# Second adder of a four-part kernel: four pairs of taps summed on VectorE, a ring of six, and side work moved to GpSimd and to the last stage

## The reference

```python
x = x + L0_conv(ln_c(x))        # 1x1 conv, adder 1x1, bn, relu, 3x3 conv, adder 3x3, bn, relu
t = t + L0_ffn(ln_t(t))         # a scan of up to 33 steps, each chooses an operation by argmax
x = x + L1_conv(ln_c(x))        # two quantised 3x3 convolutions
t = t + L1_ffn(ln_t(t))         # spectral filters (16 of them), mixed by M_phi, and M_u terms
```

```python
# out[n,co,h,w] = -sum over ci and 9 taps of |x_patch - w[co,ci,kh,kw]|
for kh in range(3):
    for kw in range(3):
        xs = xp[:, :, kh:kh + 28, kw:kw + 28]
        acc = acc - jnp.abs(xs[:, None] - w[None, :, :, kh, kw, None, None]).sum(axis=2)
```

## Time and profile before

| | |
|---|---|
| median of 3 runs | 366.26 us (362.93 to 367.12) |
| span of the profiled execution | 364.3 us; no time of its own beside the span is given for it |
| median less span | 2.0 us |
| PE busy | 346.7 us (95%) |
| DVE busy | 215.8 us (59%) |
| ACT busy | 178.7 us (49%) |
| POOL busy | 21.2 us (6%) |
| second adder, from the first unit to PE's last matmul | 39.07 to 138.54 us |
| last part, PE's filters and mixing | from 258.5 us to the end |

### The profile page before, as it was taken

The page is one execution under the profiler, slowest core; times in us unless marked ns, Lnnn a source line. Parts: engine busy times, 40 slices in busy tenths (PEclk is TensorE's granted clock), DMA queues, the critical chain, the costliest instruction groups (busy, mean ns, idle before and its releaser), DMA issues.

```text
span 364.3 us, 11456 instructions
## 1 busy us (share of the span) xinstructions
PE 346.7 (95%) x5077; PEld 212.4 (58%) x5077; DVE 215.8 (59%) x329; ACT 178.7 (49%) x180; POOL 21.2 (6%) x44
## 2 busy tenths in 40 slices
PE   8899999999999999899999998698999999999996
PEld 6437457743333345554663343465777778788884
DVE  2789999999999995455936785265211111111112
ACT  2862997887887952264828774312211111111110
POOL 4481000000000002000000000000000000000000
PEclk9999999999999999999989999999999999999999
DMA  5718300000000006400000000000230000000001
GB/s 171 222 21 266 122 2 2 2 3 2 2 2 0 2 2 234 137 7 12 1 2 2 3 1 2 7 0 2 67 71 2 4 4 4 4 4 2 4 4 46
DMA packets 10320, 13.12 MB, mean 36 GB/s; under 512 B 4106, under 2 KB 8988, under 8 KB 10264
## 3 DMA queue, kind: packets, MB, share of 16 engines
q1 hardware_dynamic: 9288, 9.11, 8.1%
q0 software_dynamic: 832, 3.00, 2.5%
q10 hardware_dynamic: 144, 0.20, 0.2%
HBM read 10.70 MB, written 0.40 MB: 30 GB/s over the span
## 4 chain that ended last, share of the span: by engine, by line
PE 57%; DVE 27%; SPq 7%; issue 4%; DMA 2%; ACT 2%; DVEq 0%; ACTq 0%
PE PS L989 57%; DVE pool_ L822 17%; SPq L238 3%; DMA W1R<-in_fwa 1%; DVE TMP L786 1%; DMA W4R<-in_aw 1%; SPq L232 1%; DVE pool_ L932 1%; DMA WA2R<-in_wa2r 1%; SPq L241 1%; SPq L243 1%; DVE pool_ L819 1%; SPq L245 1%; DVE MSC L735 0%; ACT pool_ L495 0%
## 5 line engine op out<-in xcount | busy, mean ns | idle before, releaser
L989 PE MATMUL PS<-pool_,CON 128*32 128x392 f32 (+2 forms) x1320 | 111.4, 493 | 0.7 <-ACT pool_ L495 0.2
L989 PEld LDWEIGHTS PS<-pool_,CON 128*32 128x32 f32 (+1 forms) x1320 | 49.0, 110 | 60.8 <-issue 43.7
L443 ACT ACTIVATE pool_<-TMP,WA 128x3136 f32<-128x3136 f32 x26 | 75.4, 2930 | 11.0 <-PE PS L989 10.8
L822 DVE TENSOR_SCALAR pool_<-TMP,WA 128x3136 f32<-128x3136 f32 x44 | 79.5, 1847 | 0.1
L977 DVE COPY pool_<-PS 128x392 f32<-128x392 f32 x32 | 18.1, 566 | 82.5 <-PE PS L989 82.5
L544 ACT ACTIVATE pool_<-PS 128x392 f32<-128x392 f32 x32 | 15.9, 498 | 83.3 <-PE PS L989 83.3
L989 PE MATMUL PS<-pool_,WS 128*32 128x392 f32 (+3 forms) x1024 | 46.6, 333 | 0.0
L989 PE MATMUL PS<-HE,WS 128*32 128x392 f32 (+3 forms) x1024 | 46.5, 333 | 0.1
L989 PEld LDWEIGHTS PS<-pool_,WS 128*32 128x32 f32 x1024 | 37.0, 110 | 10.0 <-issue 0.8
L989 PEld LDWEIGHTS PS<-HE,WS 128*32 128x32 f32 x1024 | 36.5, 111 | 10.7 <-issue 1.6
L989 PE MATMUL PS<-CON 128*128 128x196 f32 (+1 forms) x142 | 28.2, 337 | 1.1 <-DVE QZ L626 0.5
(11 more groups left out here) (237 smaller groups left out, 323.0 us busy)
## 6 DMA issues: line engine op xcount, KB each, us to landing
pool_<-in_pho SPq DMA_DIRECT2D x1, 3144.0 KB, 11.9
HE<-in_phe SPq DMA_DIRECT2D x1, 3136.0 KB, 11.8
QZ<-CW SPq DMA_DIRECT2D x12, 98.0 KB, 2.2
CW<-in_cw POOLq DMA_DIRECT2D x2, 576.0 KB, 4.8
CON<-in_con POOLq DMA_DIRECT2D x1, 732.5 KB, 5.6
out_y<-Y SPq DMA_DIRECT2D x1, 392.0 KB, 2.4
CQ<-in_ws SPq DMA_DIRECT2D x16, 9.0 KB
MPP<-in_mpp POOLq DMA_DIRECT2D x1, 256.0 KB, 3.1
```

Source lines behind the costliest of these rows:

```text
L443: a.activation(unit, window(n // CQ), ACT.Abs, bias=WA2[:, n:n + 1], scale=-1.0).then_inc(s["act_unit"], 1)
L822: v.tensor_scalar(unit, window(n // CQ), WA2[:, n:n + 1], None, ALU.max).then_inc(s["dve_unit"], 1)
L989: return t.matmul(out_, lhsT, rhs, start=start, stop=stop, skip_group_check=True)
```

## The change

Nine taps by eight groups were 72 groups; now c8 = 7 of taps 0 and 1, 2 and 3, 4 and 5, 6 and 7 are summed on DVE into one unit each, so PE sums 68 groups (n = 0..67). The pair stands where the odd tap's c8 = 7 stood, at n = 14, 29, 44 and 59. DVE makes the first tap's unit as before (L831 of the changed kernel), waits for it (`pair_half`), and then adds max(x, w) of the second tap in place with one `scalar_tensor_tensor` for each image (L834, 128 x 784). The second adder's ring has six slots, the sixth in `QZ`. Off DVE go: `u_mixers` and `mixers(1, .)` to DVE's own evictions of the last part (u = 1 to 9), `biases`, `quantised` and the key table to POOL; ACT's last quantising step goes to POOL and its `MUL` copies into the last part (u = 16). Steps 4 and 5 of `mixers(0, .)` move from ahead of the second adder into it (n = 10, 12).

```diff
+RG2 = 6
-NG = CQ + 9 * CQ
-ON_ACT = [on_scalar(g % CQ) for g in range(NG)]
+PAIRED = CQ - 1
+PAIRS = {1: 0, 3: 2, 5: 4, 7: 6}
+GROUPS = [((0,), c8) for c8 in range(CQ)]
+GROUPS += [((PAIRS[tap], tap) if c8 == PAIRED and tap in PAIRS else (tap,), c8)
+           for tap in range(9) for c8 in range(CQ) if not (c8 == PAIRED and tap in PAIRS.values())]
+NG = len(GROUPS)
+ON_ACT = [on_scalar(c8) for taps, c8 in GROUPS]
...
-        AMF = HSUM[:, 0:NOPS * NB]; KEYT = sb("KEYT", [P, NOPS * NB])
+        AMF = sb("AMF", [P, NOPS * NB]); KEYT = sb("KEYT", [P, NOPS * NB])
...
+        def slot(g):
+            n = g % RG if g < CQ else (g - CQ) % RG2
+            return RING[:, n, :, :] if n < RG else QZ[:, :, :]
...
# GpSimd, behind the padding of Y2R
+            g.wait_ge(s["mask_in"], 32)
+            gl(g.tensor_copy(AMF[0:1, :], AMT[0:1, :]))
+            gl(g.tensor_scalar(KEYT[0:1, :], FMT[0:1, :], 2.0, None, ALU.mult))
+            gl(g.tensor_tensor(KEYT[0:1, :], KEYT[0:1, :], AMF[0:1, :], ALU.add))
+            gl(g.tensor_scalar(AMF[0:1, :], KEYT[0:1, :], 0.0, None, ALU.is_gt))
+            gl(g.tensor_tensor(per_op(AMF), per_op(AMF), b4, ALU.mult))
+            g.tensor_tensor(per_op(KEYT), per_op(KEYT), per_op(AMF), ALU.add).then_inc(s["key_ready"], 1)
             g.wait_ge(s["ring_free"], NG)
             g.memset(H1P[:, :], 0.0).then_inc(s["pads"], 1)
+            g.wait_ge(s["decided"], 1)
+            g.wait_ge(s["q_sc"], 1)
+            for src, dst, i in ((CW1, CQ1, 0), (CW2, CQ2, 1)):
+                gl(g.tensor_scalar(src[:, :], src[:, :], QS[:, 2 + i:3 + i], 1.0, ALU.mult, ALU.mult))
+                gl(g.tensor_scalar(src[:, :], src[:, :], 127.0, -128.0, ALU.min, ALU.max))
+                gl(g.tensor_scalar(src[:, :], src[:, :], 1.0, MAGIC, ALU.mult, ALU.add))
...
+                g.tensor_scalar(dst[:, :], src[:, :], -MAGIC, 1.0, ALU.add, ALU.mult).then_inc(s["cq_done"], 1)
...
# VectorE, second adder
-            for step in range(6):
+            for step in range(4):
                 mixers(0, step)
...
+                if n in (10, 12):
+                    mixers(0, 4 + (n - 10) // 2)
-                if n == 20:
+                if n == 24:
                     widest()
-                if n == 32:
+                if n == 39:
                     scales()
-                if n in (14, 26, 38, 50):
-                    box((n - 14) // 12)
+                if n in (20, 35, 50, 63):
+                    box((20, 35, 50, 63).index(n))
...
                 if not ON_ACT[g]:
-                    v.wait_ge(s["ring_free"], g - RG + 1)
+                    if n >= RG2:
+                        v.wait_ge(s["ring_free"], g - RG2 + 1)
...
+                    else:
+                        v.tensor_scalar(unit, window(taps[0]), WA2[:, at[0]:at[0] + 1], None, ALU.max).then_inc(s["pair_half"], 1)
+                        v.wait_ge(s["pair_half"], sorted(PAIRS).index(taps[1]) + 1)
+                        for b in range(NIMG):
+                            last = v.scalar_tensor_tensor(unit[:, b], window(taps[1])[:, b], WA2[:, at[1]:at[1] + 1], unit[:, b], ALU.max, ALU.add)
+                        last.then_inc(s["dve_unit"], 1)
...
# VectorE, last part, behind the eviction of u
+                if u < 7:
+                    mixers(1, u - 1)
+                    mixers(1, u)
+                elif u < 11:
+                    u_mixers(u - 7)
+                    u_mixers(u - 6)
...
# TensorE, last part
             def mixed(grp):
+                if grp < 2:
+                    t.wait_ge(s["d_chain"], 9 * grp + 9)
```

More of the change, by code:

```diff
@@ L418, in _ @@
             a.wait_ge(s["w_a_in"], 64)
-            for n in range(9 * CQ):
+            for n in range(NG - CQ):
                 g = CQ + n
+                (tap, *_), c8 = GROUPS[g]
                 if n == CQ:
@@ L544, in _ @@
                 a.activation(UEV[:, u % 8, :], bank(u % 6), ACT.Copy).then_inc(s["uev_act"], 1)
+                if u == 16:
+                    a.wait_ge(s["u_mixed"], 4)
+                    for lag in range(3):
+                        q = slice(32 * lag, 32 * lag + 32)
+                        a.activation(MUL[q, :, :], MUS[q, :, C * lag:C * lag + C], ACT.Copy).then_inc(s["d_ready"], 1)
         @block.vector
@@ L1081, in group @@
                     for b in range(NIMG):
-                        last = mm(PS[32 * b:32 * b + 32, 6 + h, 0:HT], SEL[ON_ACT[g]][:, g % CQ, :], half(RING[:, g % RG, b, :], h), fresh, False)
+                        last = mm(PS[32 * b:32 * b + 32, 6 + h, 0:HT], SEL[ON_ACT[g]][:, GROUPS[g][1], :], half(slot(g)[:, b, :], h), fresh, False)
                         if final and 4 * h + b < 7:
@@ L1124, in _ @@
                     mm(PS[:, 1, 0:2], con_("ones", P, 1), WRW[0:1, :]).then_inc(s["wmx_bc"], 1)
-                if n == 9 * CQ - 1:
+                if n == NG - CQ - 1:
                     t.wait_ge(s["xs9_ready"], 1)
```

96 lines of the change are left out of this document (33 added, 63 removed).

## The result

The changed kernel takes 368.33 us (median of 4 runs, 366.84 to 370.95) against 364.61 us (4 runs, 362.93 to 367.12): a ratio of 1.0099, with a 95% interval of 1.0058 to 1.0139. It is slower by 1%, where I forecast 365.8 us and no change; that forecast started from before's median of three runs, 366.3, so as a change it was -0.5 us, and measured is +3.7.

The account below looks back on a forecast made before the run. PE was taken to bound the last 23 us, DVE with PE level ahead of that. Adder's end -0.8, start +0.2 and scan +0.1 gave -0.5 us: 366.3 to 365.8 us, range 361.6 to 369.4.

Parts of the forecast that it names:

- The start: Ahead of the second adder: POOL's key table costs DVE 1.0 us, two L740 taken away give 0.75; +0.2 us.
- POOL blocks DVE ahead of the adder: Rival, 5 in 100: DVE stands still for POOL's six key-table operations, adder 4.7 us later; +4.0, 370.3 us.
- The clock: Rival, 5 in 100, most inside 1%: PE's clock falls in the new waits at the pairs, some 2 us; 367 us.
- The added operation: In each pair's second half on DVE: one `scalar_tensor_tensor` costs 0.96 us start to start, 0.89 to 1.07.
- DVE's sum: DVE's work in the second adder, 93.2 us, changes by +0.74 us; its last unit ends at 133.0.
- PE's end: End of second adder: 137.7 against 138.54, -0.8 us; 4.5 of 5.3 us saved return as DVE waits, last at n = 63.
- The ring's sixth slot buys nothing: Second adder: no gain from the sixth slot, since a full ring never held DVE, only ACT.
- The quantiser: On POOL from the first decision: done in 60 us, hidden before its need at 240.9; +0.1 us for DVE in the scan.
- The tail: Behind DVE's last unit: its work shrinks, but ACT's relu behind PE's last group is waited for; nothing gained.
- The last part keeps its length: Last part: work woven in between DVE's 32 evictions makes none late; length kept to 0.2 us.
- The sum: Whole kernel: -0.8 + 0.2 + 0.1 = -0.5 us, from 366.3 to 365.8 us.

Follow-up runs that it names:

- e14: Changed kernel with the quantiser started at the second decision and 20 padding memsets ahead of DVE's work, key table still on POOL: 369.22 us, ratio 1.0101.
- e1: Changed kernel with POOL's key table begun only once the padded image is complete, beside the second adder's first units: 371.57 us, ratio 1.0205.
- e7: Changed kernel with the key table on POOL within its first 15 us, its two inputs on ACT's queue: 369.67 us, ratio 1.016.
- e4: Changed kernel with 34 instead of 18 bridging matmuls on PE ahead of the second adder: 368.62 us, ratio 1.0105.
- e17: The changed kernel itself measured once more, against the kernel before: 369.69 us, ratio 1.014.
- e10: Changed kernel, four pairs, with key table on DVE, quantiser at second decision (PE waiting for three memsets, not four) and 20 padding memsets: 364.38 us, ratio 0.9997.
- e15: The kernel of e10 with no pair instead of four: 365.48 us, ratio 0.9994.
- e11: The kernel of e10 with three pairs instead of four: 364.92 us, ratio 1.0017.
- e12: Changed kernel with the key table on DVE and 20 padding memsets, quantiser still at the first decision: 364.58 us, ratio 1.0006.
- e5: Changed kernel with only the key table back on DVE, five executions: 368.6 us, ratio 1.0131.
- e13: Changed kernel with the key table on DVE and the quantiser at the second decision, no padding memsets: 366.17 us, ratio 1.002.
- e6: Changed kernel with 20 one-column memsets ahead of DVE's work, shifting its later code: 368.27 us, ratio 1.0106.
- e16: The kernel of e5 measured once more, 12 executions: 366.97 us, ratio 1.0029.

## Why the prediction was wrong, point by point

- **The start: the step that failed.** The prediction took "1.0 us against the 0.75 us that two L740 give, +0.2 us", some 0.05 to 0.1 for a meeting. Measured: 3.0 us of holds against 0.78, two of them of 1.2 us, and a first unit 2.16 us late (42.48 - 39.07 = +3.4 in e14). I had the rule and its rival, and set the rule aside because of the earlier trace rows: there POOL copied beside plain units, and units lost 1.4%. That row was of another pairing of operations and said nothing of a chain of operations of 0.16 us each, which may stand for 1.2 us at each meeting. Nor does it hold for other POOL work beside plain units: e1.
- **The rival "POOL blocks DVE ahead of the adder"** is what came true, with 5 chances in 100. Its place is right, its size was 4.7 us at the most, found 2.16 to 3.4. Both halves of that size were off: the six operations take 8.7 us alone (e7), not 5.5, and DVE does not stand still for all of them. Its sum of 370.3 is nearer the 368.3 and 369.7 measured than my forecast, though in part for another reason, the clock.
- **The clock.** The rival for it sat in the wrong waits: not the pairs' (PE waits there for 1.4 us at most, clock 1.00) but the wait for the late first unit. It was priced at some 2 us. At its place it is 1.35 us of PE's time and 0.7 of the adder's end (e4). More is lost at 165 to 260 us in some executions, as the windows of e17 show; whether the late start makes that likelier is suggested by the counts of executions and not shown, and why it would stays open.
- **The added operation, 0.96 us start to start (0.89 to 1.07).** From the first of four to the next unit it is 3.79 us (58.65 to 62.44 in the changed kernel), 0.95 each. Right.
- **DVE's sum, 93.2 + 0.74 = 93.9.** 41.23 to 135.74 is 94.5, less the 0.68 us wait it is 93.8. Right.
- **PE's end, -0.8 us, DVE setting it, the last wait at n = 63.** Right in kind: the row at 132.35 is that wait. In size, e10 has 138.34, -0.2, but with a key cast of 0.4 us ahead of that wait and a start 0.08 later; without them it would be -0.7, an estimate. PE waits for DVE there for 3.6 us, not 4.5, the longest 1.39 at n = 44 as forecast. What the pairs bring is read from the first unit to PE's last adder matmul: 99.47 us before, 99.13 with the moved work and no pair (e15), 98.74 with three pairs (e11), 99.19 with four (e10). So **the four pairs bring nothing**, and three bring 0.4 us.
- **The ring's sixth slot buys nothing.** DVE never waited for a slot outside of the stretch of low clock; a ring of five was not tried.
- **The quantiser: hidden, +0.1 in the scan.** Hidden it is, done by 163.3. Its price is 0.06 us (e10, e12) to 0.3 (e5 against e13, 12.13 and 11.84). Right. **What had no term** was the position of DVE's code, 0.87 us (e13 against e10; 0.70 for the changed kernel against e6), which any change to the instructions ahead can bring or take.
- **The tail: nothing.** From the last adder matmul to the decision it is 9.58 us against 9.27, 9.60 in e10 and 9.59 in e15, so it is not the pairs. ACT's relu starts 0.45 us ahead of the end of PE's last group before and 0.12 ahead of it now; why is not explained.
- **The last part keeps its length.** 102.3 to 102.4 us in all kernels. Right.
- **The sum** was -0.5. With what was measured it is -0.8 + 2.16 (start) + 0.68 (DVE's wait in the slow stretch) + 0.3 (tail) + 0.87 (first FFN step, code position and quantiser together) = +3.2, against +3.4 us at the second decision. The medians moved by +3.7 and +4.9; the rest goes with the lower clock. That 368.3 still lies in the stated range is owed to the width it had been given for the rivals and for the runs' spread, not to the sum.

## What to carry to other kernels

Before moving work to GpSimd "for free", look at what DVE does at that time. A short operation on the critical path may stand for the whole of a POOL instruction (1.2 us for one of 0.16), and beside a row of large units the same six operations cost DVE twice as much (6 us in e1 against 3). A row in which two other kinds of operation got on well is no price for either. Where a rule of the hardware and a distant row disagree, give the rule more than 5 in 100. Where a kernel's executions fall on several levels of granted clock, compare them at equal clock, count how often each level comes, and don't judge 1% by five executions: e5 and e16 are the same kernel at 1.013 and 1.003.
